# Which engine issues a 16 KB transfer: the transposed maxima move from SyncE's queue to ScalarE's, with a new order table

## The reference

```python
x = _layernorm(x + _L0_attn_ref(x, ...), axis=-1)                # causal self-attention, projection
x = _layernorm(x + _L0_xattn_ref(x, ctx_1024, ctx_1024, mask, ...), axis=-1)  # cross-attention, masked
x = _layernorm(x + _L0_ffn_ref(x, ...), axis=-1)                 # attention + top-2 mixture of 8 experts

# each attention
attn = jnp.einsum('bhqd,bhkd->bhqk', q, k) * (1.0 / math.sqrt(DH))
attn = jax.nn.softmax(attn, axis=-1)
z = jnp.einsum('bhqk,bhkd->bhqd', attn, v)
# the third layer's second half
combine = jnp.sum(jax.nn.one_hot(top_i, E, dtype=x.dtype) * top_g[..., None], axis=2)
expert_out = jnp.einsum('bsd,edf->bsef', x, W_experts) + b_experts
moe_out = jnp.einsum('bsef,bse->bsf', expert_out, combine)
```

## Time and profile before

| | us |
|---|---|
| median of 3 runs | 916.08 (915.83 to 916.56) |
| the profiled execution, whole time | 917.31 |
| its span from first to last instruction | 915.5 |
| TensorE busy | 875.7 (96%) |
| VectorE busy | 767.5 (84%) |
| ScalarE busy | 587.5 (64%) |
| GpSimd busy | 427.0 (47%) |
| granted TensorE clock, mean | 0.994 |

### The profile page before, as it was taken

How to read it: one execution, slowest core, us unless ns; L and a number is a source line. 1 busy time by engine, 2 the same in 40 slices (tenths; PEclk the granted TensorE clock), 3 DMA queues, 4 the chain that set the end, 5 groups by cost and what they waited for, 6 DMA issues and landing times.

```text
span 915.5 us, 28485 instructions
## 1 busy us (share of the span) xinstructions
PE 875.7 (96%) x10018; PEld 745.9 (81%) x10018; DVE 767.5 (84%) x3508; ACT 587.5 (64%) x1211; POOL 427.0 (47%) x588
## 2 busy tenths in 40 slices
PE   7899899999999999999999999999999999999996
PEld 4688788888878888888888788888888888888874
DVE  2689787999888988888887888888888888888985
ACT  5578787888867878778787654444555544555533
POOL 7678787898774545445453322222222222222201
PEclk9999999999999999999999999999999999999999
DMA  5665565655544544444343322222222232322200
GB/s 177 171 167 164 142 177 147 165 152 152 150 114 119 149 114 117 129 115 125 107 126 92 80 54 72 83 82 83 83 83 83 82 83 83 83 81 74 78 28 25
DMA packets 98163, 100.47 MB, mean 110 GB/s; under 512 B 10701, under 2 KB 90599, under 8 KB 98023
## 3 DMA queue, kind: packets, MB, share of 16 engines
q1 hardware_dynamic: 98023, 98.66, 38.9%
HBM read 18.14 MB, written 4.19 MB: 24 GB/s over the span
## 4 chain that ended last, share of the span: by engine, by line
PE 73%; issue 7%; DMA 7%; ACT 5%; DVE 4%; SPq 1%; POOL 1%; ACTq 0%; POOLq 0%; DVEq 0%
PE work L515 38%; PE work L659 9%; PE scores L636 8%; PE max_scores L612 7%; DMA q_stack<-neg_max_t 5%; PE work L668 3%; PE scores L639 3%; ACT attn L819 2%; DMA q_stack<-q_parts 1%; PE work L540 1%; DVE max_scores L985 1%; SPq L442 1%; PE work L521 1%; ACT neg_max_t L813 1%; PE work L677 1%
## 5 line engine op out<-in xcount | busy, mean ns | idle before, releaser
L985 DVE CUSTOM_DVE_ANT_0 max_scores<-max_scores,mask_qk 128x128 f32<-128x128 f32 x872 | 223.3, 324 | 37.2 <-PE max_scores L612 37.1
L819 ACT ACTIVATE attn<-scores 128x512 f32<-128x512 f32 x384 | 215.8, 596 | 55.8 <-PE scores L636 49.2
L612 PE MATMUL max_scores<-k_stack,q_stack 126*128 126x128 bf16 x1536 | 145.8, 221 | 6.8 <-DMA q_stack<-q_parts 3.7
L636 PE MATMUL scores<-q_stack,k_stack 128*128 128x128 bf16 x1536 | 141.2, 220 | 11.2 <-DMA q_stack<-neg_max_t 7.7
L612 PEld LDWEIGHTS max_scores<-k_stack,q_stack 126*128 126x128 bf16 x1536 | 98.9, 98 | 40.2 <-issue 19.5
L1099 POOL TENSOR_TENSOR q_full<-q_full,q_parts 128x512 f32<-128x512 f32 x48 | 56.3, 1174 | 152.8 <-ACT q_parts L777 152.8
L1058 DVE SCALAR_TENSOR_TENSOR x_all<-work,combine,x_all 128x256 f32<-128x256 f32 x256 | 121.3, 479 | 6.6 <-PE work L515 1.9
L988 DVE TENSOR_REDUCE neg_max<-max_scores 128x4 f32<-128x512 f32 x166 | 112.3, 680 | 12.8 <-PE max_scores L615 9.9
L985 DVE DVE_READ_ACCUMULATOR2_ANT neg_max<- 128x1 f32 x872 | 122.9, 141 | 0.0
L636 PEld LDWEIGHTS scores<-q_stack,k_stack 128*128 128x128 bf16 x1536 | 96.7, 97 | 30.8 <-DMA q_stack<-neg_max_t 13.8
L515 PE MATMUL work<-split_hi,w_hi 128*128 128x256 f32 x384 | 115.7, 301 | 3.0 <-DVE split_lo L888 2.8
(11 more groups left out here) (125 smaller groups left out, 2098.9 us busy)
## 6 DMA issues: line engine op xcount, KB each, us to landing
k_stack<-k_parts SPq DMA_DIRECT2D x288, 128.0 KB, 2.6
q_stack<-q_parts SPq DMA_DIRECT2D x288, 128.0 KB, 2.5
in_t<-in_xt SPq DMA_DIRECT2D x16, 256.0 KB, 3.1
x_all<-in_x SPq DMA_DIRECT2D x16, 256.0 KB, 3.0
in_t<-in_ct SPq DMA_DIRECT2D x16, 256.0 KB, 3.4
out<-x_all SPq DMA_DIRECT2D x16, 256.0 KB, 2.2
stage<-in_e SPq DMA_DIRECT2D x4, 512.0 KB, 5.1
stage<-in_qk SPq DMA_DIRECT2D x2, 512.0 KB, 4.3
```

The source lines that it names most:

```text
L612: mm = pe.matmul(dst[:, b, h2, :], head(QS, n, 2 * p + h2, b, ROWS), head(KS, n, 2 * p + h2, b, ROWS), start=(b + h2 == 0), stop=(b + h2 = ...
L636: mm = pe.matmul(dst[:, b, h2, :], head(KS, n, 2 * p + h2, b, rows), head(QS, n, 2 * p + h2, b, rows), start=(b + h2 == 0), stop=(b + h2 = ...
L819: act.activation(attn("exp", n, p)[:, :, :], SS[g % 2][:, :, :, :].rearrange("k b h q -> k (b h) q"), ACT.Exp).then_inc(probs_done, 1)
L985: ins = dve.tensor_tensor_reduce(scores, scores, MQ[l][:, :], -1.0, HUGE, ALU.add, ALU.min, NM[n % 2][:, b, h:h + 1])
```

## The change

`ml` leaves SyncE's list and enters ScalarE's, behind `mt`; the wait and the transfer are the same, the queue is ScalarE's. All of `TIMES` and `SHIFTS` have new numbers, so other steps change places too. The computation is the same, instruction for instruction.

```diff
-PERIOD = [16.59, 18.07, 24.92]
+PERIOD = [16.59, 18.07, 24.89]
...
-     "zT": [11.62, 15.82], "z": [13.34, 16.94], "in": [-76.28], "xr": [-22.34], "xh": [-44.25], "xl": [-42.32],
+     "zT": [11.24, 16.14], "z": [13.12, 16.71], "in": [-75.08], "xr": [-17.88], "xh": [-48.86], "xl": [-42.67],
...
-            def max_load(n, part):
-                sp.wait_ge(mt_done, n + 1)
-                sp.dma_start(QS[n % STACKS][ROWS:ROWS + MAX_PARTS, :, :, :], MT[n % 2][:, :]).then_inc(max_stacked[n % 2], 16)
-
...
-            work = {"in": load_in, "xr": load_rows, "qs": q_stack, "ks": k_stack, "ml": max_load, "store": store,
+            work = {"in": load_in, "xr": load_rows, "qs": q_stack, "ks": k_stack, "store": store,
...
+            def max_load(n, part):
+                act.wait_ge(mt_done, n + 1)
+                act.dma_start(QS[n % STACKS][ROWS:ROWS + MAX_PARTS, :, :, :], MT[n % 2][:, :]).then_inc(max_stacked[n % 2], 16)
+
...
-                    "qm": q_middle, "km": k_middle, "gexp": gate_exps, "mt": max_t, "exp": probs, "za": z_aug, "zh": z_high, "norm": normalise}
+                    "qm": q_middle, "km": k_middle, "gexp": gate_exps, "mt": max_t, "ml": max_load, "exp": probs, "za": z_aug, "zh": z_high, "norm": normalise}
```

More of the change, by code:

```diff
@@ L60 @@
 RB_COLS = 2 * D + E
-PERIOD = [16.59, 18.07, 24.92]
+PERIOD = [16.59, 18.07, 24.89]
 TIMES = [
[4 rows of a table removed]
-     "max": [-18.73, -18.28, -13.85, -12.08, -10.39, -8.09, -5.87, -4.3], "nm": [-3.92], "maxt": [-3.48],
[4 rows of a table removed]
-     "norm": [31.53], "causal": [2.74, 3.79, 3.8, 4.61, 6.05, 8.11, 9.52, 10.06], "va": [-15.89]},
[4 rows of a table removed]
-     "max": [-16.75, -15.08, -14.32, -12.04, -11.47, -8.29, -8.01, -6.18], "nm": [-5.99], "maxt": [-2.95],
[9 rows of a table removed]
-     "max": [-26.31, -24.84, -23.6, -21.09, -16.38, -15.43, -13.63, -11.69], "nm": [-7.43], "maxt": [-6.94],
[3 rows of a table removed]
[L95 to L98, removed]
[4 rows of a table added]
+     "max": [-18.44, -17.72, -13.47, -11.29, -10.06, -7.75, -5.39, -4.21], "nm": [-3.85], "maxt": [-3.74],
[4 rows of a table added]
+     "norm": [32.94], "causal": [3.03, 4.21, 4.23, 4.93, 7.33, 8.46, 9.83, 10.37], "va": [-15.99]},
[4 rows of a table added]
+     "max": [-16.75, -15.03, -14.49, -12.25, -12.0, -8.18, -8.04, -6.22], "nm": [-6.02], "maxt": [-3.73],
[9 rows of a table added]
+     "max": [-26.3, -24.83, -22.49, -20.47, -16.26, -15.16, -13.43, -11.25], "nm": [-7.42], "maxt": [-6.66],
[3 rows of a table added]
+     "gtop": [-19.91], "gateT": [-14.89], "cbt": [-16.2], "bias": [-13.57], "eb": [-14.35],
+     "expert": [-7.36, -6.11, -4.58, 1.22, 3.11, 5.71, 6.98, 14.06],
+     "combine": [-6.04, -4.26, -2.96, 1.79, 4.38, 6.13, 9.22, 15.69], "zadd": [12.19, 21.81], "stat": [26.12],
+     "rs": [20.37], "norm": [33.24], "store": [27.33]},
 ]
 SHIFTS = {
[9 rows of a table removed]
[9 rows of a table added]
 }
```

## The result

The changed kernel takes **932.92 us** (median of 4 runs, 931.64 to 935.9), beside 916.32 for the kernel before (4 runs, 915.83 to 918.65): a ratio of 1.0171, with a 95% interval of 1.0148 to 1.0194. It is slower, as forecast, but by 16.6 us where I had forecast 5.8, and outside my range of 912 to 928. The profiled execution is the fastest of the four, 931.64 us.

What follows compares the result with a forecast made beforehand. TensorE bounds every layer, paced in layer 0 by copy, transfer, score, exponential, score. Layer 0 +5.5 (7.6 less 2.1), layer 1 +0.3, layer 2 0: +5.8 us, median 916.1 to 921.9; range 912 to 928.

Steps and rivals of the forecast that it cites:

- SyncE without the wait: 0: SyncE's queue: first `ks` transfers leave some 3 us earlier, but beyond the 2.1 us given back this changes nothing, 0.
- all of the table but `xh` at nothing: Other reordered steps: exchanged neighbours in layer 2, and the start and last item, each put at 0, give or take 0.5.
- The hop of 0.03 us, nothing to save: From ScalarE's copy to SyncE's issue costs 0.03 us, so issuing on the engine that made the data saves nothing.
- h = 0.5 us: Layer 0: what ScalarE loses per item because the issue holds its queue, 0.5 us, with bounds of nothing and 1.0.
- The second rival: Layer 0: the issue waits until the copy `za` has ended, h = 1.0; +12.0 us, 928.1; chance 0.12.
- Item 11: Layer 0's pattern item: first exponential 3.8 us after the copy of the maxima; copy to copy 14.45 becomes about 15.0.
- `xh`: Layer 0, items 0 to 11: this copy moves ahead of the first exponential, adding 0.5 us, with 0.47 free in some items.
- The 2.1 us given back: Layer 0: TensorE's 2.1 us of waits for late q stack transfers would all go, subtracted from a 7.6 us loss.
- The third rival (lands sooner): The transfer and stacks land before TensorE asks: -6.3 us, 909.8, or -3, 913, with half lost to `xh`; chance 0.20.
- Layer 1, +0.3: Issue hidden in idle time before `qe`, 0.6 to 0.9 left; `qm` costs 0 to 0.1 in 11 items, 0.3 in all.
- Layer 2, 0: ScalarE idle 3.11 us behind the copy, so the issue is free; TensorE's neighbours exchanged: 0, give or take 0.5.

Runs made afterwards that it cites:

- b: The changed kernel's new table alone, against the kernel before; SyncE still issues the 16 KB transfer behind its wait: 922.41 us, ratio 1.0048.
- m: The new table with SyncE issuing the real transfer, plus a needless 512-byte issue on ScalarE, against the kernel before: 930.24 us, ratio 1.0118.
- f: The kernel before, plus ScalarE waiting for its copy of the maxima and issuing a needless 512-byte transfer: 926.59 us, ratio 1.0094.
- a: The kernel before with its old table, only the 16 KB issue moved from SyncE to ScalarE directly behind the copy of the maxima: 931.43 us, ratio 1.0141.
- k: The new table with SyncE issuing, and layer 0's `xh` copy back behind the fourth exponential, against the kernel before: 921.75 us, ratio 1.0048.
- d: The changed kernel with layer 0's `xh` copy back behind the fourth exponential: 929.93 us, ratio 1.0145 to the kernel before.
- c: The changed kernel with SyncE waiting again for the copy of the maxima, ScalarE still issuing: 945.11 us, ratio 1.0300 to the kernel before.
- i: The changed kernel with SyncE held until ScalarE's 16 KB transfer has landed: 951.1 us, ratio 1.0377 to the kernel before.
- j: The kernel before with the issue alone moved to ScalarE and SyncE held until the 16 KB transfer has landed: 930.18 us, ratio 1.0134.
- n: The changed kernel with SyncE held until the landing in items 1, 2 and 6 alone: 932.45 us, ratio 1.0151 to the kernel before.
- l: The kernel before with the issue moved to ScalarE in layer 2 alone: 917.51 us, ratio 1.0006.
- e: The kernel before with one wait added on ScalarE directly behind its copy of the maxima, issuing nothing: 920.42 us, ratio 1.0024.
- h: The kernel before with the new table in layer 2 alone, SyncE issuing everywhere: ratio 0.9995.
- g: The kernel before with ScalarE waiting for its copy and issuing a needless 16 KB transfer: 926.27 us, ratio 1.0076.

## Why the prediction was wrong

The sign was right, and so was one of the mechanisms, ScalarE's held queue; the time was outside the range. **Two steps failed: "SyncE without the wait: 0", and all of the table but `xh` at nothing.** The loss (16.6 us by the medians, 15.7 by the ratio 1.0171), divided by the ratios of b, m and the changed kernel: **table 0.5% (4 us), ScalarE's queue held by an issue of 512 bytes 0.7% (6 us), the real transfer on another queue than SyncE's 0.5% (5 us)**. Each of these steps has an error of about 0.2 to 0.3%, and the last holds the 1 to 1.5 us of the longer issue. Laid against the sum, the profiled layer 0 grew by 11.2 us where I had 5.5, layer 1 by 4.6 where I had 0.3, and layer 2 shrank by 1.7 where I had 0.

- *The hop of 0.03 us, nothing to save.* Right: ScalarE's issue starts as soon behind the copy.
- *h = 0.5 us.* Right in kind, a little high: 0.62 us of issue instead of 0.67, the next step 0.11 us behind its end instead of 0.22, and h 0.37 to 0.39 in the changed order. My terms with h in layer 0 come to 4.5 us; m has 2.6 there over b, with its shorter issue. That run f's layer 0 paid 5.5 us, as much as my sum for the layer, is chance: it has the old table and a loss of 0.73 us an item. The second rival, `za` waited for, is wrong for this table; directly behind the copy, as in a, the loss is 0.85, since there the queue also waits for its own copy.
- *Item 11.* First exponential 3.63 us behind the copy, where I said 3.8; TensorE 74.66 busy from 120 to 200, where I said 74.5; that is in part luck, since the late landing of item 6 (130.56, 3.53 us), which I had not in my sum, lies in this stretch. From copy to copy it was 15.38 and not 15.0. Run b, without the issue, has 15.00 already, by a weight copy that I took for unmoved (argued, as said under b). From item 11's copy to item 12's it was 15.58, where I had `xh` and the issue cancel.
- *`xh`.* Over-sized: about 3.1 us in my sum, 0.4 to 1.4 measured (k, d).
- *The rest of the table in layer 0.* Missing: b has 4.4 us there, of which `xh` is the small part. I had counted the issue and `xh` and let all other exchanges pass at nothing. The length behind item 11's copy has 1.1 of them, with TensorE's wait of 0.94 at the second transpose, and the one ahead of it 0.5, with the weight copy; what causes the wait, and the rest of these 4 us, stays open.
- *The 2.1 us given back.* Wrong: the waits for late q stacks rose from 3.7 to 4.6 us in the whole span, and in the stretch that I took them from, from 2.1 to 2.7.
- *SyncE without its wait costs nothing.* This step failed. I looked for what lands sooner, and not for what it would meet. The transfers that SyncE no longer holds back share the DMA engines with the 16 KB (run a item 6; items 1, 2, 6 of the changed kernel). That company makes the landings late is shown by b, c and i. That late landings make the 5 us is not: j and n took most of them away and the time did not come back. What was there in their place is known in part: the longer issue, late stacks in j, item 4's landing in n, and TensorE's clock, which fell twice in layer 0 of either profiled execution.
- *The third rival (lands sooner)* is wrong in sign. The rule that the prediction cites from the Trainium skill ("DMA: Bandwidth & Descriptors", section "Issuing engines are not separate DMA queues"), that transfers from several engines end on the same DMA engines, was the right guide, but I read it as "gains 0"; in c sharing them makes the landing 1.1 us later (3.48 for 2.35 us in the item shown).
- *Layer 1, +0.3.* Measured +2.6 against the unchanged l, +4.6 against the short profile. The item that I took as pattern did hide the issue: `qe` starts 1.94 us behind the copy as before, and the 1.57 us that the view shows ahead of it still count the issue as idle time, so the 0.6 to 0.9 that I named could not show there. But not every item has idle time behind its copy. In item 18 a weight copy stands there (run a shown; the changed kernel has the same), and the length to item 19 is 16.87 us beside 16.05 in b:

```profile
316.88 0.65 ACTq L820 DMA_DIRECT2D q_stack<-neg_max_t  x1
317.63 1.06 ACT L735 ACTIVATE w_hi<-stage 128x1024 fp32r<-128x1024 f32 x1 [0.78 <-ACT neg_max_t L809]
```

The larger part is the table's: behind the copies of items 16, 29 and 31 the changed kernel is 1.0, 0.6 and 0.7 us longer than l, and b, where SyncE issues, is 1.4, 0.4 and 0.8 longer. The idle time behind the copy covered the issue in items 19 to 29; that the new order costs nothing at the ends of the layer was wrong.

- *Layer 2, 0.* The issue is free there (l). The table gained 1.7 us (b: 2.0), beyond my half microsecond: an exchange of neighbours on TensorE is worth something, 0.18 us an item.

## What to carry to other kernels

An issue moved off a waiting engine also takes that wait away: ask which transfers it held back, and which of them will now be in flight beside the one that is waited for. In this kernel the small transfer that others wait for was best placed first in the same queue as the large ones, directly behind the event that releases them. Price the held queue at every place where the issue goes, not at one item as pattern: here it was free where the engine was idle behind it (layer 2), and 0.4 us behind one other step or 0.85 directly behind the copy where it was not. A profile is one execution: look at the clock of every stretch before a longer length is put down to the change.

## What the runs showed of the hardware

Two queues that start at the same moment: 16 KB land after 3.15 to 3.76 us beside 256 KB of another queue (21 of 24 landings in c), and after 2.27 to 2.45 us when they are first in one queue (b).

ScalarE's wait for its own copy costs 0.13 us by itself, since steps otherwise overlap (e), 0.73 with an issue of 0.50 us (f), and 0.85 with one of 0.62 (a).

TensorE's clock fell in some executions and not in others at the same place. In runs a, f, j and m, behind item 31, it ran in part at the lower level of 1.2 GHz (in h too, some 2 us sooner after the copy). In a and f it had been idle for 1.6 us of the 4 ahead, as in the kernel before, which kept its clock. Run a (the column after POOL is the granted clock):

```profile
534.00:538.00 4.00, 2.38 (x18) 1.94 (x18) 2.31 (x6) 1.49 (x4) 1.01 (x1) 0.92 0.37 98
538.00:542.00 4.00, 4.00 (x32) 2.83 (x31) 2.86 (x8) 2.03 (x4) 0.17 (x1) 0.66 0.00 0
```

The same place before:

```profile
520.00:524.00 4.00, 2.38 (x22) 1.60 (x21) 3.44 (x12) 2.68 (x6) 1.15 (x1) 1.00 0.33 83
524.00:528.00 4.00, 4.00 (x50) 3.15 (x51) 2.71 (x8) 2.27 (x5) 0.42 (x1) 1.00 0.05 15
```

From item 31 to 32 runs a, f and j took 18.27, 18.16 and 18.12 us, where l took 16.42; m took 18.55, where b took 17.19. In a and f the gate's exponentials came 0.7 to 0.8 us later than before. Run g had them as late as f, kept the clock (1.00) and took 16.54, so the delay alone does not decide it, and no run here shows what does.

Over all executions, the mean granted clock was 0.9918 in the four of the changed kernel and 0.9944 in the 56 of the kernel before that were made beside runs a to n. Taken as time lost, the share missing to 1 is 7.7 us of 933 and 5.1 of 917: an estimate, from these means, of up to 2.6 us of the 16.6 that went by the clock. It is inside the three parts given under "Why the prediction was wrong" and not beside them.
